# Statistics of the residual one tile per pair, and five other pieces of work at other places, in a four-layer kernel on one core

## The chip, the core and the metric

The kernel runs on one NeuronCore of a Trainium2 chip. The core has a matrix engine (TensorE; PE in the profile, its weight loads PEld), a vector engine (VectorE, DVE), an activation engine (ScalarE, ACT), a general engine (GpSimd, POOL), and the queue of the sync engine (SP), which here issues every DMA. The metric is the time of one execution on the device, in microseconds (us), as the median of the runs shown. Before the change it is 844.3 us.

## The reference

The input is 2 sequences of 512 tokens, 512 wide. Each of four layers adds its normed output to the residual x:

```
x = x + ln(mamba(ln(x)))       # projections to 1024, causal conv of 4 taps, selective scan with 16 states, @ W_out.T
x = x + ln(ffn16(ln(x)))       # gate, up and down weights packed in 4 bits, 1376 inner columns, silu(gate) * up
x = x + ln(attention(ln(x)))   # 16x16 scores of each token, one key and value head
x = x + ln(moe(ln(x)))         # shared expert relu(.)^2 with up and down, and a routed product
# ln(a) = (a - mean(a)) / sqrt(var(a) + 1e-5) along the 512 columns
```

The second layer dequantizes its weights: `w = q * s - (z + 1) * s`, q from `(word >> 4 * (row % 8)) & 15`, with scales s and zero points z of groups of 128 rows.

## The kernel before

A sequence ("half", b = 0 or 1) has four tiles of 128 tokens (t = 0 to 3). There is no scheduler: each engine runs the list of instructions that is written out for it, and semaphores tie the lists together. Four tables or positions in loops set the order. In PSUM four banks hold sums or decays, one holds the scan's output, and three are a ring that all other products of TensorE (items such as `("out", 1, 3)`) go through in one order, so that an item waits until the one three before it has been taken.

**The scan stage** (about 60 to 494 us of the profile) runs 128 pairs. Pair i belongs to chunk cc = i // 8 (128 of the 1024 channels of one half; 16 chunks) and to q = i % 8 in it. For each pair

- ScalarE writes two exponentials of 128x512 to PSUM (`decay`, line 1708), once VectorE is through with pair i-2, whose banks they take;
- GpSimd multiplies `rep_du` by `bc` into `dbu` (line 2142, three buffers), after the scan three pairs back;
- VectorE scans over both (line 1104), and multiplies the states by C (line 1115); for two or three pairs of eight GpSimd does that product (line 2151);
- TensorE sums the states of two pairs (line 881).

Other work is put behind certain pairs. On ScalarE these are copies from PSUM, the steps of the next chunks' dt (lines 1672 to 1678) and, once `out` of half 0 is there, layer norms: behind pairs 90 and 91 `sums(t)` (line 1733) goes over two tiles each of the residual x, with the row sum by the accumulator; behind pair 92 comes `less_mean`, and behind 92 and 93 `squares` (line 1739) of two tiles each; behind 94 `own_root`. Each `sums(t)` waits until GpSimd has added the normed tile to x (line 2180), which it does for two tiles behind pair 87 and for two behind pair 89. `norm_ffn` reads the result behind pair 103.

**The end of the scan stage.** The product with W_out for half 1 has 8 terms, one per chunk. Its first 6 are summed during the scan (`("part", t)`, t = 0 to 3; ScalarE copies them to `obuf`), and the last 2 behind the last scan (`("out", 1, t)`), where VectorE adds both (line 1407).

**The FFN of half 0** (about 505 to 607 us) has 11 steps of 128 inner columns. In step i TensorE does `g` and `u` (12 f16 products of 128x512 each, since operands are split in a high and a low f16 part), and then the 12 products of `down(i-1)`. `g` waits for the weights of step i (`wlo_gu`), `down` for `it_lo` of its step. At the same time VectorE and ScalarE make the weights of the steps to come out of loads of 1.5 MB each (`stage`, four slots; the first three issue freely, `stage(3)` when `("out", 1, 3)` is computed, and `stage(i)` from 4 on when the weights of step i-4 are made). VectorE does in step i: `it` = silu(g) * u (line 1299); unpack of step i+3 (line 1147, waits for its load); `it_lo` (line 1309, waits for the high part from ScalarE); the low weights of step i+2 (lines 1162 and 1164, after ScalarE's high part); scaling for step i+3 (lines 1154 and 1156). At the end of step 0 stand the statistics of the normed `out` of half 1 (lines 1047 and 1050), and at the end of step 4 those of the new residual; at the end of steps 8 to 10 stands the low part of a transposed tile of half 1 (`low_turned`, line 1172). ScalarE does in step i: silu, high part of `it`, high weights of i+2, cast for i+3, then the high part of a transposed tile (`high_turned`, line 1778) and, in steps 1 and 5, the root of the statistics with a table load before and after. TensorE transposes tile t of half 1 at the end of step 7+t (line 652), into the ring bank that the tile before it must have left.

The FFN of half 1 with the attention of half 0 follows (607 to about 703 us), and then the last layer.

Of the kernel before, what the change touches and what calls it, by code (L numbers as in the profile page):

```python
# [48 lines left out]
LOG_EXP = "natural_log_exp_and_others"  # L49

# [37 lines left out]
PARTS = DC - 2  # L88
# [71 lines left out]
def build(nc, x_in, ident_in, meanmat_in, shift_in, shifts_in, w_in, conv_in, par_in, alog_in, wx_in, wdt_in,  # L160
# [15 lines left out]
    with ExitStack() as ctx:  # L176
# [274 lines left out]
        def wait_taken(eng, item):  # L451

            eng.wait_ge(taken_sem(item), ring(item)[1] + 1)
# [184 lines left out]
        def _(pe):  # L638
# [111 lines left out]
            def out_partial(t):  # L750

                item = ("part", t)
                pe.wait_ge(y_taken, DC + PARTS)
                start(item)
                product(item, [(u0[:, c, t * P:(t + 1) * P], wout[:, c, :]) for c in range(PARTS)])\
                    .then_inc(work_ready, 1)

            def out_part(b, t):
# [4 lines left out]
                               for c in range(PARTS * b, DC)])\  # L763
# [271 lines left out]
        def _(dve):  # L1035
# [384 lines left out]
            for i in range(IC):  # L1420
# [5 lines left out]
                ffn_low(0, i)  # L1426
                if i == 2:
# [13 lines left out]
                if i == 0:  # L1441
                    for t in range(NT):
                        wait_taken(dve, ("out", 1, t))
                    stats(("out", 1), [obuf[1][:, t, :] for t in range(NT)])
                if i == 4:
                    dve.wait_ge(out_done, NB * NT)
                    stats(("ffn", 1), x_tiles(1))
                if i > TURN_FIRST:
                    low_turned(1, [i - TURN_FIRST - 1])
# [119 lines left out]
        def _(act):  # L1569
# [287 lines left out]
            for i in range(NPAIR):  # L1857
# [75 lines left out]
                if i in (last + 12, last + 13):  # L1933
                    sums(2 * (i - last - 12))
                    sums(2 * (i - last - 12) + 1)
                if i == last + 14:
                    less_mean()
                    squares(("ffn", 0), 0, x[:, 0, :])
                    squares(("ffn", 0), 1, x[:, 1, :])
                if i == last + 15:  # L1940
                    squares(("ffn", 0), 2, x[:, 2, :])
                    squares(("ffn", 0), 3, x[:, 3, :])
# [4 lines left out]
                if i == last + 16:  # L1947
                    own_root(("ffn", 0), fnmr, fnmr_ready)
# [52 lines left out]
            act.wait_ge(exp_done, NPAIR)  # L2001
            whole(0)
# [4 lines left out]
            for k in range(NB * IC):  # L2007
                b, i = divmod(k, IC)
                ffn_silu(k)
                ffn_high(k)  # L2010
                if k + 2 < IC:
                    high_weights(k + 2)
                if k + 3 < IC:
                    whole(k + 3)
                if TURN_FIRST < k < IC:
                    high_turned(1, [k - TURN_FIRST - 1])
# [293 lines left out]
```

## Time and profile before

| | us |
|---|---|
| median of 3 runs | 844.3 (842.31 to 845.25) |
| profiled execution, its own time | 844.68 |
| its span, first to last instruction | 842.8 |
| TensorE products busy | 692.8 (82%) |
| VectorE busy | 691.4 (82%) |
| GpSimd busy | 493.8 (59%) |
| ScalarE busy | 460.0 (55%) |
| mean granted TensorE clock | 0.904 of full speed |

All times below are of that profiled execution, counted from the start of its span. 1.9 us of its own time lie outside the span. The shares are means over stages of different kinds. A row of a timeline has the start, the busy time and the instruction; what stands in brackets is how long the engine sat idle before it, and whose work ended that.

### The profile page before, as it was taken

The page shows a single profiled execution, that of the slowest core. Times are in us where ns is not written, and L with a number is a line of the kernel's source. Part 1 is how long each engine was busy: PE and PEld are TensorE (multiplying, and loading weights), DVE is VectorE, ACT ScalarE, POOL GpSimd, SP SyncE. Part 2 cuts the span into 40 slices and gives each one's busy share as a digit, 9 for nine tenths or more (in the row PEclk, how much of TensorE's full clock was granted, in tenths as well). Part 3 has the DMA queues.
Part 4 walks back from the last instruction along what each step waited for, and adds up shares of the span by engine and source line. Part 5 has one row for each costly group of instructions (what it writes and reads, how often), then busy time and mean ns, then how long its engine had stood idle before and what let it go on. Part 6 is the DMA issues. An engine that isn't in the chain of part 4 may idle for free. (4 is left out here: it accounts for less than half of the span.)

```text
span 842.8 us, 8287 instructions
## 1 busy us (share of the span) xinstructions
PE 692.8 (82%) x2732; PEld 320.0 (38%) x2732; DVE 691.4 (82%) x700; ACT 460.0 (55%) x772; POOL 493.8 (59%) x258
## 2 busy tenths in 40 slices
PE   5989679998777879366648868997999999999993
PEld 4533123332222323011112223433444546787882
DVE  5779899999999999979999989997265564586668
ACT  3556687797655765856555434765334346323421
POOL 1319999989999999999998920210002005340151
PEclk9999879999968999756858979999999999999998
DMA  9224312331535524533127029870040030000011
GB/s 289 49 74 158 118 37 95 126 124 65 185 103 182 168 75 138 176 124 113 38 100 222 28 76 236 227 210 18 1 150 1 0 100 2 1 0 1 1 51 50
DMA packets 40945, 82.39 MB, mean 98 GB/s; under 512 B 6711, under 2 KB 8160, under 8 KB 40648
## 3 DMA queue, kind: packets, MB, share of 16 engines
q1 hardware_dynamic: 40904, 81.87, 31.0%
q8 instruction: 22, 0.36, 0.2%
q14 instruction: 19, 0.16, 0.1%
HBM read 70.65 MB, written 11.21 MB: 97 GB/s over the span
## 5 line engine op out<-in xcount | busy, mean ns | idle before, releaser
L2142 POOL TENSOR_TENSOR dbu<-rep_du,bc 128x1024 f32<-128x1024 f32 x128 | 299.6, 2366 | 2.3 <-ACT rep_du L1837 1.4
L1708 ACT ACTIVATE psum<-rep_dt,aneg 128x512 f32<-128x512 f32 x256 | 166.2, 682 | 125.2 <-DVE hc L1115 104.8
L1104 DVE TENSOR_TENSOR_SCAN psum<-psum,dbu 128x1024 f32<-128x1024 f32 x87 | 198.8, 2285 | 10.2 <-ACT psum L1708 9.7
L881 PE MATMUL psum<-hc,stk 128*32 128x512 f32 x512 | 87.5, 762 | 58.8 <-POOL hc L2151 30.4
L1115 DVE TENSOR_TENSOR hc<-psum,bc 128x1024 f32<-128x1024 f32 x87 | 106.5, 1224 | 3.4 <-PE psum L881 0.4
L2151 POOL TENSOR_TENSOR hc<-hc,bc 128x1024 f32<-128x1024 f32 x41 | 96.8, 2360 | 8.6 <-DVE hc L1104 8.5
L1104 DVE TENSOR_TENSOR_SCAN hc<-psum,dbu 128x1024 f32<-128x1024 f32 x41 | 93.5, 2281 | 4.7 <-PE psum L881 2.8
L658 PE MATMUL psum<-xf_hi,gu_hi 128*128 128x512 f16 x176 | 67.4, 383 | 1.5 <-ACT sg L1982 1.0
L658 PE MATMUL psum<-xf_hi,gu_lo 128*128 128x512 f16 x176 | 67.2, 382 | 0.0
L658 PE MATMUL psum<-xf_lo,gu_hi 128*128 128x512 f16 x176 | 67.2, 382 | 0.0
L873 PE MATMUL psum<-u,diag 128*32 128x512 f32 x128 | 24.6, 851 | 42.3 <-DVE u L1131 22.9
L881 PEld LDWEIGHTS psum<-hc,stk 128*32 128x32 f32 x512 | 12.9, 122 | 116.7 <-issue 68.4
L2220 POOL TENSOR_TENSOR h<-h 128x512 f32<-128x512 f32 x16 | 19.3, 1208 | 64.5 <-ACT h L2070 63.8
L658 PE MATMUL psum<-xT,w_g 128*128 128x512 f32 x112 | 56.4, 652 | 0.3 <-DVE dt_t L1123 0.3
L1299 DVE TENSOR_TENSOR it<-sg,psum 128x512 f32<-128x512 f32 x22 | 15.1, 685 | 44.3 <-issue 24.8
L1989 ACT CAST it_hi<-it 128x512 f16<-128x512 f32 x22 | 13.6, 620 | 54.6 <-DVE it L1299 54.6
L2184 POOL TENSOR_TENSOR x<-x,obuf 128x512 f32<-128x512 f32 x4 | 8.2, 2076 | 52.2 <-ACT obuf L1766 52.2
L2191 POOL TENSOR_TENSOR w_gate_lo<-w_gate,w_gate_hi 128x32 fp32r<-128x32 f32 x1 | 0.7, 695 | 64.3 <-ACT w_gate_hi L2038 64.3
L2204 POOL TENSOR_TENSOR w_up_lo<-w_up,w_up_hi 128x1024 fp32r<-128x1024 f32 x4 | 9.4, 2378 | 47.4 <-ACT w_up_hi L1974 47.4
L906 PE MATMUL psum<-d_hi,it_hi 128*128 128x512 f16 x88 | 33.3, 379 | 4.6 <-DVE it_lo L1309 4.6
L658 PEld LDWEIGHTS psum<-xT,w_g 128*128 128x128 f32 x112 | 22.4, 208 | 36.4 <-issue 35.1
L658 PE MATMUL psum<-xT,w_x 128*128 128x512 f32 x64 | 31.4, 637 | 3.2 <-ACT u L1636 1.8
(256 smaller groups left out, 1444.5 us busy)
## 6 DMA issues: line engine op xcount, KB each, us to landing
rep_dt<-rep_scratch SPq DMA_DIRECT2D x60, 256.0 KB, 3.3
rep_du<-rep_scratch SPq DMA_DIRECT2D x60, 256.0 KB, 4.2
cw<-c_scratch SPq DMA_DIRECT2D x11, 768.0 KB, 9.4
qw<-qgu_in SPq DMA_DIRECT2D x11, 512.0 KB, 5.3
bc<-bc_scratch SPq DMA_DIRECT2D x16, 256.0 KB, 4.8
rep_scratch<-du_t SPq DMA_DIRECT2D x15, 256.0 KB, 2.0
rep_scratch<-dt_t SPq DMA_DIRECT2D x15, 256.0 KB, 2.3
qw<-qd_in SPq DMA_DIRECT2D x11, 256.0 KB, 7.0
```

The costliest lines, as they stand in the source:

```text
L658: last = pe.matmul(bank(item)[0:rows, cols], lhsT, rhs, start=(n == 0), stop=(n == len(parts) - 1))
L873: last = pe.matmul(y_rows(k), diag[:, k * P // KH:(k + 1) * P // KH], u[b][:, c, :], start=True, stop=False)
L881: last = pe.matmul(y_rows(k), stk[:], hc[:, (i + k // 2) % HCS, k % 2, :], start=False, stop=(s == GN - 1))
L906: last = pe.matmul(psum[:, t, :], v, w, start=(i == 0 and n == 0), stop=(i == IC - 1 and n == 2))
L1104: dve.tensor_tensor_scan(h, a, dbu[:, i % DBS].rearrange("p e t -> p (e t)"), 0.0, ALU.mult, ALU.add)\
L1115: dve.tensor_tensor(hc[:, i % HCS], psum[:, two, :], bc[:, GN + n, :].unsqueeze(1).broadcast_to([P, 2, L]), ALU.mult)\
L1299: dve.tensor_tensor(it[:, k % 2, :], sg[:, k % 2, :], bank(("u", b, i)), ALU.mult)\
L1708: last = act.activation(psum[:, 2 * (i % 2) + e, :], rep_dt[:, cc % 2, k, :], ACT.Exp, scale=aneg[:, k, c, n:n + 1])
L1989: act.copy(it_hi[:, k % 2, :], it[:, k % 2, :]).then_inc(ithi_done, 1)
L2142: pool.tensor_tensor(dbu[:, i % DBS], rep_du[:, cc % 2, k:k + 2, :], bc[:, n, :].unsqueeze(1).broadcast_to([P, 2, L]), ALU.mult).then_inc( ...
L2151: pool.tensor_tensor(hc[:, i % HCS], hc[:, i % HCS], bc[:, GN + n, :].unsqueeze(1).broadcast_to([P, 2, L]), ALU.mult)\
L2220: pool.tensor_tensor(h2[:, k % 2, :], h1[:, k % 2, :], h1[:, k % 2, :], ALU.mult)\
```

## The change

Six pieces of work get another place; only a load of ScalarE's function table is made explicit, and nothing is computed in another way.

1. In the scan stage ScalarE's `sums` go one tile per pair behind pairs 91 to 94, `less_mean` and the `squares` one tile per pair behind 95 to 98, and `own_root` behind 99.
2. `("part", 3)` sums 7 of the 8 terms, and `("out", 1, 3)` the last one alone. The other three tiles keep 6 and 2.
3. ScalarE loads the table set with silu right after the last exponential of the scan stage, and not before the first silu.
4. VectorE's statistics of `out` (half 1) move from the end of step 0 of the FFN to behind `it_lo` of step 1, and those of the residual from the end of step 4 to behind `it_lo` of step 5.
5. `low_turned` of VectorE moves from the end of its step to behind `it_lo`.
6. `high_turned` of ScalarE moves ahead of the high weights.

```diff
-PARTS = DC - 2
+
+
+def parts_of(t):
+
+    return DC - 1 if t == NT - 1 else DC - 2
...
                 ffn_low(0, i)
+                if i > TURN_FIRST:
+                    low_turned(1, [i - TURN_FIRST - 1])
+                if i == 1:
+                    for t in range(NT):
+                        wait_taken(dve, ("out", 1, t))
+                    stats(("out", 1), [obuf[1][:, t, :] for t in range(NT)])
+                if i == 5:
+                    dve.wait_ge(out_done, NB * NT)
+                    stats(("ffn", 1), x_tiles(1))
                 if i == 2:
...
                     scaled(i + 3)
-                if i == 0:
-                    for t in range(NT):
-                        wait_taken(dve, ("out", 1, t))
-                    stats(("out", 1), [obuf[1][:, t, :] for t in range(NT)])
-                if i == 4:
-                    dve.wait_ge(out_done, NB * NT)
-                    stats(("ffn", 1), x_tiles(1))
-                if i > TURN_FIRST:
-                    low_turned(1, [i - TURN_FIRST - 1])
...
-                if i in (last + 12, last + 13):
-                    sums(2 * (i - last - 12))
-                    sums(2 * (i - last - 12) + 1)
-                if i == last + 14:
-                    less_mean()
-                    squares(("ffn", 0), 0, x[:, 0, :])
-                    squares(("ffn", 0), 1, x[:, 1, :])
-                if i == last + 15:
-                    squares(("ffn", 0), 2, x[:, 2, :])
-                    squares(("ffn", 0), 3, x[:, 3, :])
+                if last + 13 <= i < last + 13 + NT:
+                    sums(i - last - 13)
+                if last + 17 <= i < last + 17 + NT:
+                    t = i - last - 17
+                    if t == 0:
+                        less_mean()
+                    squares(("ffn", 0), t, x[:, t, :])
...
-                if i == last + 16:
+                if i == last + 21:
                     own_root(("ffn", 0), fnmr, fnmr_ready)
...
             act.wait_ge(exp_done, NPAIR)
+            act.preload_act_table_set(SILU)
             whole(0)
...
                 ffn_high(k)
+                if TURN_FIRST < k < IC:
+                    high_turned(1, [k - TURN_FIRST - 1])
                 if k + 2 < IC:
                     high_weights(k + 2)
                 if k + 3 < IC:
                     whole(k + 3)
-                if TURN_FIRST < k < IC:
-                    high_turned(1, [k - TURN_FIRST - 1])
```

(`last` is 78, `TURN_FIRST` is 7.) The line numbers of the changed program are 6 or 7 higher at the places below, and those of its VectorE rows 7 higher.

ScalarE's list behind pairs 89 to 94. The `psum<-rep_dt,aneg` rows are the exponentials, two for a pair; `spare,asum<-x` is a `sums`, `spare,avar<-x` a `squares`, `dt_t`, `diag` and `w1t` are work that stays. Before:

```order
L1708 ACTIVATE psum<-rep_dt,aneg 128x512 x6
L1733 ACTIVATE spare,asum<-x 128x512 x2
L1708 ACTIVATE psum<-rep_dt,aneg 128x512 x2
L1672 ACTIVATE dt_t<-psum 128x512
L1733 ACTIVATE spare,asum<-x 128x512 x2
L1708 ACTIVATE psum<-rep_dt,aneg 128x512 x2
L1683 ACTIVATE diag<-ident,par 128x128
L1675 ACTIVATE dt_t<-dt_t 128x512
L1736 ACTIVATE nmean<-asum 128x4
L1739 ACTIVATE spare,avar<-x,nmean 128x512 x2
L1708 ACTIVATE psum<-rep_dt,aneg 128x512 x2
```

With the change:

```order
L1715 ACTIVATE psum<-rep_dt,aneg 128x512 x8
L1679 ACTIVATE dt_t<-psum 128x512
L1740 ACTIVATE spare,asum<-x 128x512
L1715 ACTIVATE psum<-rep_dt,aneg 128x512 x2
L1690 ACTIVATE diag<-ident,par 128x128
L1682 ACTIVATE dt_t<-dt_t 128x512
L1740 ACTIVATE spare,asum<-x 128x512
L1715 ACTIVATE psum<-rep_dt,aneg 128x512 x2
L1685 ACTIVATE dt_t<-dt_t 128x512
L1857 COPY w1t<-psum 128x512
L1740 ACTIVATE spare,asum<-x 128x512
```

Between the exponentials of pairs 91 and 92, where two `sums` stood, now stands one, and it is that of the first tile.

VectorE's list from the end of step 0 of the FFN of half 0 (`w_132` is the scaled weight of step 3). Before:

```order
L1156 TENSOR_TENSOR w_132<-cw_136 128x1536
L1047 BN_STATS bst<-obuf_111 128x6 x4
L1050 BN_AGGR mv<-bst 128x2 x4
L1299 TENSOR_TENSOR it<-sg,psum 128x512
L1147 TENSOR_SCALAR qw_125<-qw_125,shift 128x1536
L1309 TENSOR_TENSOR it_lo<-it,it_hi 128x512
L1162 TENSOR_TENSOR gu_lo<-w_132,gu_hi 128x1024
```

With the change:

```order
L1163 TENSOR_TENSOR w_132<-cw_136 128x1536
L1306 TENSOR_TENSOR it<-sg,psum 128x512
L1154 TENSOR_SCALAR qw_125<-qw_125,shift 128x1536
L1316 TENSOR_TENSOR it_lo<-it,it_hi 128x512
L1054 BN_STATS bst<-obuf_111 128x6 x4
L1057 BN_AGGR mv<-bst 128x2 x4
L1169 TENSOR_TENSOR gu_lo<-w_132,gu_hi 128x1024
```

The eight instructions of the statistics stood ahead of `it`, the unpack and `it_lo` of step 1; now they stand behind these and ahead of the low weights of step 3. The same happens in steps 4 and 5.

VectorE's list in step 8 (`xf_lo` is the low part of the transposed tile 0). Before:

```order
L1299 TENSOR_TENSOR it<-sg,psum 128x512
L1309 TENSOR_TENSOR it_lo<-it,it_hi 128x512
L1162 TENSOR_TENSOR gu_lo<-w_131,gu_hi 128x1024
L1164 TENSOR_TENSOR d_lo<-w_131,d_hi 128x512
L1172 TENSOR_TENSOR xf_lo_142<-psum,xf_hi_140 128x4x128
```

With the change:

```order
L1306 TENSOR_TENSOR it<-sg,psum 128x512
L1316 TENSOR_TENSOR it_lo<-it,it_hi 128x512
L1179 TENSOR_TENSOR xf_lo_142<-psum,xf_hi_140 128x4x128
L1169 TENSOR_TENSOR gu_lo<-w_131,gu_hi 128x1024
L1171 TENSOR_TENSOR d_lo<-w_131,d_hi 128x512
```

`xf_lo` passes the two instructions of the low weights; `xf_hi` on ScalarE passes the two of the high weights in the same way. In steps 9 and 10 no weights are left to be made, and the rows stand as before.

## Rows read from the trace of the kernel before

**Rows 1.** The page, part 1: busy us, share of the span and instructions of each engine.

```profile
PE 692.8 (82%) x2732; PEld 320.0 (38%) x2732; DVE 691.4 (82%) x700; ACT 460.0 (55%) x772; POOL 493.8 (59%) x258
```

**Rows 2.** Windows: start:end and length, busy us (instructions), clock, DMA share, GB/s.

```profile
361.00:395.00 34.00, 20.64 (x56) 4.90 (x54) 28.55 (x18) 22.47 (x48) 33.89 (x18) 0.65 0.28 99
395.00:493.70 98.70, 64.18 (x230) 18.80 (x230) 97.98 (x62) 50.32 (x82) 90.81 (x42) 0.76 0.30 99
607.30:646.30 39.00, 37.64 (x177) 17.11 (x175) 24.49 (x47) 15.91 (x26) 3.42 (x3) 1.00 0.22 81
646.30:807.00 160.70, 157.56 (x763) 109.78 (x764) 99.72 (x185) 66.00 (x118) 40.65 (x30) 1.00 0.05 15
```

**Rows 3.** Timeline of VectorE: the scans of pairs 91 to 94.

```profile
368.11 2.30 DVE L1104 TENSOR_TENSOR_SCAN psum<-psum,dbu 128x1024 f32<-128x1024 f32 x1 [0.48 <-POOL dbu L2142]
...
374.95 2.30 DVE L1104 TENSOR_TENSOR_SCAN psum<-psum,dbu 128x1024 f32<-128x1024 f32 x1 [3.29 <-ACT psum L1708]
...
379.07 2.29 DVE L1104 TENSOR_TENSOR_SCAN hc<-psum,dbu 128x1024 f32<-128x1024 f32 x1 [0.56 <-ACT psum L1708]
...
382.85 2.30 DVE L1104 TENSOR_TENSOR_SCAN psum<-psum,dbu 128x1024 f32<-128x1024 f32 x1 [0.91 <-ACT psum L1708]
```

**Rows 4.** Timeline of ScalarE: the third of the sums, and a read of the accumulator.

```profile
371.64 0.63 ACT L1733 ACTIVATE spare<-x 128x512 f32<-128x512 f32 x1 [3.29 <-POOL x L2180]
372.17 0.19 ACT L1733 ACTIVATION_READ_ACCUMULATOR spare<-x 128x1 f32 x1
```

**Rows 5.** Timeline of GpSimd behind the residual's additions.

```profile
372.73 2.35 POOL L2151 TENSOR_TENSOR hc<-hc,bc 128x1024 f32<-128x1024 f32 x1
375.03 6.98 POOL L2142 TENSOR_TENSOR dbu<-rep_du,bc 128x1024 f32<-128x1024 f32 x3
```

**Rows 6.** Timeline of TensorE: last W_out products, step 1's g, down(1), transpose of tile 1.

```profile
496.65 8.78 PE L658 MATMUL psum<-wout,u 128*128 128x512 f32 x16 [0.81 <-DVE u L1131]
...
511.05 0.39 PE L658 MATMUL psum<-xf_hi,gu_hi 128*128 128x512 f16 x1 [0.43 <-DVE gu_lo L1162]
...
527.38 0.38 PE L906 MATMUL psum<-d_hi,it_hi 128*128 128x512 f16 x1 [1.52 <-DVE it_lo L1309]
...
585.14 0.97 PE L652 MATMUL psum<-ident,obuf 128*128 128x128 f32 x4 [4.40 <-DVE xf_lo L1172]
```

**Rows 7.** Timeline of VectorE in the FFN of half 0, steps 0 to 2.

```profile
516.16 1.02 DVE L1147 TENSOR_SCALAR qw<-qw,shift 128x1536 int32<-128x1536 int32 x1 [0.62 <-DMA cw<-c_scratch]
...
522.10 2.46 DVE L1047 BATCH_NORM_STATS2 bst<-obuf 128x6 f32<-128x512 f32 x4
...
525.01 0.69 DVE L1299 TENSOR_TENSOR it<-sg,psum 128x512 f32<-128x512 f32 x1
...
526.55 0.69 DVE L1309 TENSOR_TENSOR it_lo<-it,it_hi 128x512 f16<-128x512 f32 x1
527.34 1.23 DVE L1162 TENSOR_TENSOR gu_lo<-w,gu_hi 128x1024 f16<-128x1024 f32 x1
...
532.99 0.69 DVE L1299 TENSOR_TENSOR it<-sg,psum 128x512 f32<-128x512 f32 x1 [1.01 <-ACT sg L1982]
```

**Rows 8.** Timeline of VectorE in step 8: low parts of it and of tile 0.

```profile
581.76 0.69 DVE L1309 TENSOR_TENSOR it_lo<-it,it_hi 128x512 f16<-128x512 f32 x1 [0.74 <-DVE it L1299]
...
584.40 0.68 DVE L1172 TENSOR_TENSOR xf_lo<-psum,xf_hi 128x512 f16<-128x512 f32 x1
```

**Rows 9.** Timeline of ScalarE: the table load before the first silu, and xf_hi of tile 0.

```profile
510.27 1.28 ACT L1982 ACT_TABLE_LOAD   x1
...
583.05 0.58 ACT L1778 CAST xf_hi<-psum 128x512 f16<-128x512 f32 x1
```

**Rows 10.** DMA issues of 508 to 509 us: the last transfer of stage(4), us to landing.

```profile
cw<-c_scratch SPq DMA_DIRECT2D x1, 768.0 KB, 14.6
```

**Rows 11.** Windows, TensorE alone: length, busy us, granted clock, DMA share, GB/s.

```profile
406.00:411.70 5.70, 3.03 (x13) 1.00 0.00 0
585.10:588.70 3.60, 3.56 (x11) 0.53 0.00 0
```

More of the change, by code:

```diff
@@ L49 @@
 LOG_EXP = "natural_log_exp_and_others"
+SILU = "silu_and_others"
 POOL_C = ((1, 4, 6), (2, 5))
@@ L752, in out_partial @@
                 item = ("part", t)
-                pe.wait_ge(y_taken, DC + PARTS)
+                pe.wait_ge(y_taken, DC + parts_of(t))
                 start(item)
-                product(item, [(u0[:, c, t * P:(t + 1) * P], wout[:, c, :]) for c in range(PARTS)])\
+                product(item, [(u0[:, c, t * P:(t + 1) * P], wout[:, c, :]) for c in range(parts_of(t))])\
                     .then_inc(work_ready, 1)
@@ L762, in out_part @@
                 product(item, [(gated[b][:, c, t * P:(t + 1) * P], wout[:, c, :])
-                               for c in range(PARTS * b, DC)])\
+                               for c in range(parts_of(t) * b, DC)])\
                     .then_inc(work_ready, 1)
```

## The prediction

> **What bounds the kernel now.** I read the page first. TensorE and VectorE are both busy for 82% of the span [rows 1], so no engine bounds it as a whole and the stages have to be read apart. The windows do that. From 395 to 494 us, in the scan stage, VectorE works for 97.98 of 98.70 us and GpSimd for 90.81: VectorE bounds, with GpSimd 8% behind. From 361 to 395 us it is the other way round: GpSimd 33.89 of 34.00 us, VectorE only 28.55 [rows 2]. That is where the moved statistics of the residual stand. From 607 us on TensorE is the bound, 37.64 of 39.00 us and 157.56 of 160.70 [rows 2]. So whatever is gained before 607 us should reach the end whole, and the change touches nothing behind it.
>
> The waits in the two stages that it does touch are next. In the scan stage the scans of pairs 92, 93 and 94 begin 3.29, 0.56 and 0.91 us late, each for ScalarE's exponentials [rows 3]; 4.8 us in all. The reason is in ScalarE's own list: the third of its `sums` sat 3.29 us until GpSimd had added tile 2 to the residual [rows 4], and the exponentials of pair 92 were queued behind it. In the FFN of half 0 TensorE waits for VectorE: 1.52 us before `down(1)`, and once more the same before `down(5)`, both right behind moved statistics, and 4.40 us before the transpose of tile 1 [rows 6].
>
> **The change part by part.**
>
> *Residual statistics in the scan stage.* The same eight passes are done (0.63 us and a read of 0.19 us for one of the sums [rows 4]), so the work is unchanged and only what queues behind it differs. Behind pair 91 there is now one sum, of tile 0, which has long been added. The sums of tiles 2 and 3 come behind pairs 93 and 94, later than 372.73 us, when GpSimd is through with its additions [rows 5]. None waits. A pair takes VectorE 2.2 us or, with the product by C, 3.5 us; ScalarE has its exponentials and one pass in 2.1 us, so it keeps up. The 4.8 us of waits for ScalarE go. What is late next is GpSimd: the `dbu` of pair 93 is the first of the three that begin at 375.03 and take 6.98 us together, so it is there at 377.4 [rows 5]. The scan of pair 93 began at 379.07 [rows 3], and can begin 1.6 us earlier, not 4.3. From there the scan (2.2) and a short step of VectorE (0.6) follow, so pair 94 starts at 380.3 instead of 382.85 [rows 3]: 2.5 us earlier. Behind it GpSimd has some 8% of room [rows 2], and followed through its list it comes within 0.1 us of holding the scans up once more. I take **2.4 us**. The bounds are 0 (if GpSimd gives nothing back) and 4.8 (if it has room that I don't see). `own_root` comes five pairs later and still four pairs ahead of its reader; it costs nothing.
>
> *One term of the W_out product of tile 3.* The eight products behind the last scan take 8.78 us [rows 6]. The first two run at half rate, so with six at full rate one of these costs 8.78 / 10 = 0.9 us. Moved ahead, it stands in `("part", 3)` in a place where TensorE then idles for some 4 us, and its chunk has long been taken: hidden. Behind the scan it saves TensorE 0.9 us, but `g` of step 1 waits for its low weights at 511.05 in any case [rows 6], so TensorE itself gains nothing. It has another effect: `stage(3)` is issued when this product is done. VectorE's unpack in step 0 waited for just this load until 516.16 [rows 7], and now has it 0.9 us earlier. The gain is **0.9 us**, with 0 as the lower bound if the transfers land no earlier.
>
> *The table load.* 1.28 us go from before the first silu [rows 9]. VectorE would then have `it` of step 0 some 0.6 us earlier, but it waits for the load at 516.16 a little later [rows 7], which hides this: 0 now, 0.6 if that cover were gone.
>
> *Statistics one step later.* They are 2.46 us and the 0.4 behind it: 2.9 us, from 522.10 to the `it` at 525.01 [rows 7]. Without them, and with the 0.9 from above, this `it` starts 3.8 us earlier, at 521.2. The unpack behind it then meets the load of `stage(4)`, issued between 508 and 509 us and landed 14.6 us later, so at 523.2 [rows 10], or 522.4 with the 0.9; it waits 0.6 us. `it_lo` is ready for `down(1)` when TensorE comes, and the 1.52 us of [rows 6] are gone. Then the 2.9 us of statistics follow, and behind them the low weights of step 3, for which TensorE now waits some 0.8 us. On VectorE's chain two things are removed: the 1.01 us before the `it` at 532.99 [rows 7], where ScalarE had to wait for the statistics and then load two tables, and about 0.3 us of short gaps such as that between `it_lo` at 526.55 and the low weights at 527.34, where 0.6 would do [rows 7]. One thing is added, the 0.6 us for the load. Net 0.7. In steps 4 and 5 the same is done with loads that land early: net 1.3. Together **2.0 us**. Bounds: 0, if TensorE's wait for `it_lo` only becomes one for weights, and 3.0, both waits of 1.52.
>
> *The turned tile.* Transpose 1 needs tile 0's ring bank, and this is free when `xf_lo` at 584.40 is through; between it and `it_lo` at 581.76 stand two low-weight instructions [rows 8]. The next start behind `it_lo` is 0.6 us after it, 582.4: **2.0 us** earlier. `xf_hi` has to be there by then; it was at 583.05 [rows 9], behind two casts of 1.5 us which it now passes. The low weights of step 10 come 0.6 us later, more than 10 us ahead of their use. The bounds are 1.5 and 2.0.
>
> *The clock.* Behind that wait of 4.40 us [rows 6] TensorE was granted 0.53 of its clock for 3.60 us [rows 11], the lower of its two levels (1.2 and 2.4 GHz) nearly throughout, which loses 1.7 us. The wait now is 2.4 us. In the window from 406 to 411.7 us TensorE idled for 2.7 us at a stretch, and the granted clock stayed at 1.00 [rows 11]. So I expect it not to fall: **1.7 us**. The bounds are 0 and 1.7. The Trainium skill (TensorE: Matmul & The Clock Gate, the section on the clock gate) says that half rate is the default and that activity, watched in windows that run freely, releases it. By that rule the moment is a matter of chance between executions: the sum would be 1.7 us less in a run where a window falls badly.
>
> The sum is 2.4 + 0.9 + 2.0 + 2.0 + 1.7 = 9.0 us. From the profiled execution's own 844.7 us this gives 835.7; the median of the runs is 0.4 lower, so **835.3 us**.
>
> **The rivals.**
>
> - *GpSimd has more room than I see*, and the scan stage gives all 4.8 us: 835.3 - 2.4 = 832.9 us. Against it stands 33.89 of 34.00 us.
> - *The scan stage gives nothing*, as GpSimd takes the place of ScalarE or the nine passes hold up exponentials of the short pairs: 837.7. For it speaks that one pass and two exponentials nearly fill a pair of 2.2 us.
> - *The clock falls all the same* at 580 us: 837.0. A single pair of numbers speaks against it.
> - *The transfers don't come earlier.* Four are in flight together there, and the load of step 4 took 14.6 us. If the loads bound steps 0 to 2, the 0.9 goes and with it some 0.4 of the first statistics: 836.6.
> - *The statistics now delay the weights by as much*: 837.3.
> - *Slower: TensorE falls to 1.2 GHz in the dense part.* The change makes TensorE's work arrive otherwise, and a stretch of T us at the lower level loses T / 2. From 607 us on the windows show 1.00 throughout [rows 2]. To eat the 9.0 us it takes 18 us of such a stretch, and at 27 us the time is 848.8 us. Nothing in the profile hints at it.
> - *The change does nothing measurable*: the waits are named wrongly, 844. In the scan stage the exponentials' wait is plain, so this needs GpSimd to have been the true cause there as well as in the FFN.
>
> **How the numbers follow.** Chances: my forecast 42 in 100; full gain in the scan stage 8; none there 11; the clock falls 17; the transfers 12; weights delayed 4; slower 3; nothing 3. Two of the lesser misses together reach 839.4, and the best case with a little off is 832. The range is 832.0 to 839.5 us. 0.3% (2.5 us) is about what a measurement of this kernel can tell from no change. All cases but the last two are faster by more: faster 0.94, same 0.03, slower 0.03.
>
> **What would show it.** In the profile after: the scan of pair 92 without a wait, that of pair 93 waiting for GpSimd's `dbu` by 1 to 3 us; the last scan 2.4 us earlier; the unpack of step 0 still waiting for its load, but 0.9 us earlier counted from the last scan; no wait of TensorE for `it_lo` before `down(1)` and `down(5)`, and one under 1 us for low weights before the `g` behind each; TensorE's wait before the transpose of tile 1 down to 2.4 us, and the clock at 1.00 behind it. From 607 us on the stages should be as long as before. I would be wrong if the wait of pair 93 for `dbu` repeats in the pairs that follow, if the transfers of `stage(4)` and `stage(5)` end the waits in steps 1 and 2, or if later stages, which I take over unchanged, give something back.

## The result and the profile after

The changed kernel takes **837.64 us** (median of 4 runs, 835.98 to 837.94), against 844.41 (842.31 to 845.25) for the kernel before on the same chip: a ratio of 0.9923, 95% interval 0.9909 to 0.9937. That is 6.8 us less, where 9.0 were forecast; 837.64 lies in the range of 832.0 to 839.5 and 2.3 us above the point of 835.3. Its profiled execution took 837.52 us with a span of 835.7, so 7.1 us less in the span. The mean granted clock is 0.901 (before 0.904). The ratio is estimated over all runs of both kernels and is not the quotient of the two medians (0.9920 here), so a difference taken from ratios can be up to 1 us away from one taken from medians; below it is said where medians were used.

The page's first part, to be held against [rows 1]: the same work to within 1.5 us on each engine.

```profile
PE 691.4 (83%) x2732; PEld 320.0 (38%) x2732; DVE 690.6 (83%) x700; ACT 459.2 (55%) x772; POOL 493.4 (59%) x258
```

The windows over the same stretches as in [rows 2] (columns as there). VectorE's busy time from 361 to 395 us rose from 28.55 to 30.95: the 2.4 us that it sat idle less. GpSimd is as full there as it was. In the last stage, taken over 161.0 us where it was 160.7, TensorE is busy for 157.91 us where it was 157.56, at a clock of 1.00 in both.

```profile
361.00:395.00 34.00, 20.47 (x64) 4.78 (x62) 30.95 (x20) 22.83 (x45) 33.93 (x19) 0.70 0.29 95
...
639.00:800.00 161.00, 157.91 (x764) 109.73 (x765) 99.76 (x185) 65.96 (x118) 40.80 (x30) 1.00 0.05 16
```

VectorE's scans of pairs 91 to 94, which answer to [rows 3]. The 3.29, 0.56 and 0.91 us for ScalarE are gone, and one wait of 2.36 us for GpSimd stands before pair 93.

```profile
368.29 2.30 DVE L1111 TENSOR_TENSOR_SCAN psum<-psum,dbu 128x1024 f32<-128x1024 f32 x1 [0.49 <-POOL dbu L2147]
371.76 2.29 DVE L1111 TENSOR_TENSOR_SCAN psum<-psum,dbu 128x1024 f32<-128x1024 f32 x1
377.67 2.29 DVE L1111 TENSOR_TENSOR_SCAN hc<-psum,dbu 128x1024 f32<-128x1024 f32 x1 [2.36 <-POOL dbu L2147]
380.45 2.29 DVE L1111 TENSOR_TENSOR_SCAN psum<-psum,dbu 128x1024 f32<-128x1024 f32 x1
```

GpSimd's rows to [rows 5]: its list starts 0.2 us later, as the whole program does in this execution, and is otherwise unmoved. Pair 94 thus starts 2.40 us earlier than before, or 2.6 us counted from that later start.

```profile
375.22 6.97 POOL L2147 TENSOR_TENSOR dbu<-rep_du,bc 128x1024 f32<-128x1024 f32 x3
```

Four more rows of VectorE before the change are wanted as marks: the product of the last scan stage, the add of `("out", 1, 1)`, `it` of step 0 and `it` of step 6.

```profile
495.91 0.69 DVE L1131 TENSOR_TENSOR u<-u,psum 128x512 f32<-128x512 f32 x1 [1.13 <-PE psum L881]
...
502.04 0.69 DVE L1407 TENSOR_TENSOR obuf<-psum,obuf 128x512 f32<-128x512 f32 x1 [1.02 <-PE psum L658]
...
512.19 0.69 DVE L1299 TENSOR_TENSOR it<-sg,psum 128x512 f32<-128x512 f32 x1 [0.60 <-ACT sg L1982]
...
566.57 0.69 DVE L1299 TENSOR_TENSOR it<-sg,psum 128x512 f32<-128x512 f32 x1 [1.01 <-ACT sg L1982]
```

The same marks after, with the rows that answer to [rows 7]:

```profile
493.71 0.69 DVE L1138 TENSOR_TENSOR u<-u,psum 128x512 f32<-128x512 f32 x1 [1.13 <-PE psum L888]
...
501.03 0.69 DVE L1414 TENSOR_TENSOR obuf<-psum,obuf 128x512 f32<-128x512 f32 x1 [2.07 <-PE psum L665]
...
510.50 0.68 DVE L1306 TENSOR_TENSOR it<-sg,psum 128x512 f32<-128x512 f32 x1
...
513.76 1.02 DVE L1154 TENSOR_SCALAR qw<-qw,shift 128x1536 int32<-128x1536 int32 x1
...
519.69 0.68 DVE L1306 TENSOR_TENSOR it<-sg,psum 128x512 f32<-128x512 f32 x1
520.29 1.01 DVE L1154 TENSOR_SCALAR qw<-qw,shift 128x1536 int32<-128x1536 int32 x1
521.22 0.68 DVE L1316 TENSOR_TENSOR it_lo<-it,it_hi 128x512 f16<-128x512 f32 x1
...
529.14 0.68 DVE L1306 TENSOR_TENSOR it<-sg,psum 128x512 f32<-128x512 f32 x1
...
561.27 0.68 DVE L1306 TENSOR_TENSOR it<-sg,psum 128x512 f32<-128x512 f32 x1
```

TensorE's rows to [rows 6]. The 1.52 us before `down(1)` is gone (so is that before `down(5)`), and no wait for weights stands behind it. The wait before the transpose of tile 1 fell from 4.40 to 2.37.

```profile
494.45 9.12 PE L665 MATMUL psum<-wout,u 128*128 128x512 f32 x14 [0.81 <-DVE u L1138]
...
510.04 0.39 PE L665 MATMUL psum<-xf_hi,gu_hi 128*128 128x512 f16 x1 [1.29 <-DVE gu_lo L1169]
...
523.29 0.38 PE L913 MATMUL psum<-d_hi,it_hi 128*128 128x512 f16 x1
...
577.79 0.65 PE L659 MATMUL psum<-ident,obuf 128*128 128x128 f32 x4 [2.37 <-DVE xf_lo L1179]
```

Taking the starts of the same instructions from each other gives where the time came from:

| up to | shift | the step |
|---|---|---|
| `u` at 493.71 | -2.20 | scan stage -2.4, and 0.2 later from the start |
| add at 501.03 | -1.01 | **+1.2 given back** in the W_out products |
| `it` of step 0 at 510.50 | -1.69 | -0.7, of it 0.60 the wait for `sg` |
| unpack at 513.76 | -2.40 | -0.7, of it 0.62 the wait for the load |
| `it` of step 2 at 529.14 | -3.85 | -1.45, first statistics |
| `it` of step 6 at 561.27 | -5.30 | -1.45, second statistics |
| transpose 1 at 577.79 | -7.35 | -2.05, turned tile |
| end | -7.1 | nothing for the clock; 0.2 lost near 700 us |

The windows of TensorE alone for its two stretches at half clock (columns as in [rows 11]): around the W_out products, and behind the transpose of tile 1.

```profile
486.60:500.20 13.60, 9.62 (x23) 0.50 0.34 84
578.70:582.10 3.40, 3.40 (x9) 0.50 0.00 0
```

The same of before, around the W_out products:

```profile
489.80:500.00 10.20, 7.04 (x20) 0.50 0.21 53
```

Both stretches at half clock end near 500 us, though the products now start 2.2 us earlier. Of the time behind that start 3.35 us lay at 1.2 GHz before (496.65 to 500.0) and 5.75 us now (494.45 to 500.2). These are 2.4 us more, and at half clock they cost half of that, the 1.2 us given back in the table. The products of seven terms, 14 recorded ones, take 9.12 us where those of eight, 16 recorded ones, took 8.78 [rows 6].

### The profile page after: what moved, and what is told of

The parts are those of the page before. It is cut to its first block and busy times, and to the rows that moved or that the text cites. A ratio compares the mean times of both kernels' runs of the same rounds, so it can differ in the third digit from the quotient of the medians.

```text
span 835.7 us, 8289 instructions
## 1 busy us (share of the span) xinstructions
PE 691.4 (83%) x2732; PEld 320.0 (38%) x2732; DVE 690.6 (83%) x700; ACT 459.2 (55%) x772; POOL 493.4 (59%) x258
## 5 line engine op out<-in xcount | busy, mean ns | idle before, releaser
L888 PE MATMUL psum<-hc,stk 128*32 128x512 f32 x512 | 85.2, 743 | 60.8 <-POOL hc L2156 37.7
L1993 ACT CAST it_hi<-it 128x512 f16<-128x512 f32 x22 | 13.6, 618 | 51.9 <-DVE it L1306 51.9
```

The source lines that it names most:

```text
L888: last = pe.matmul(y_rows(k), stk[:], hc[:, (i + k // 2) % HCS, k % 2, :], start=False, stop=(s == GN - 1))
```

## Experiments

Twelve kernels were run, each beside the kernel before on the same chip. The diffs show the core of each edit.

### One item at a time

Item 1 alone, the statistics of the residual one tile per pair:

```diff
-                if i in (last + 12, last + 13):
-                    sums(2 * (i - last - 12))
-                    sums(2 * (i - last - 12) + 1)
+                if last + 13 <= i < last + 13 + NT:
+                    sums(i - last - 13)
```

> The kernel before with the residual statistics of the scan stage one tile per pair, and nothing else. My theory, that GpSimd ends the wait that ScalarE ended: the scan of pair 93 waits some 2.4 us for dbu, the last scan ends 2.4 us earlier than in the kernel before, and the time falls by 1.0 to 2.4 us, less where TensorE's clock is low in the W_out products behind the scans. Rival, ScalarE's passes were the whole cause: no wait for dbu, 4.8 us less.

Measured: 843.8 us (842.1 to 844.76, 12 runs) against 843.86 (30 runs), ratio 0.9999 (0.9988 to 1.0009). VectorE's timeline shows the waits gone as in the full change:

```profile
367.01 2.30 DVE L1104 TENSOR_TENSOR_SCAN psum<-psum,dbu 128x1024 f32<-128x1024 f32 x1 [0.51 <-POOL dbu L2139]
370.49 2.29 DVE L1104 TENSOR_TENSOR_SCAN psum<-psum,dbu 128x1024 f32<-128x1024 f32 x1
376.40 2.29 DVE L1104 TENSOR_TENSOR_SCAN hc<-psum,dbu 128x1024 f32<-128x1024 f32 x1 [2.37 <-POOL dbu L2139]
```

This execution was 1.1 us ahead at pair 91 (367.01 against 368.11 in [rows 3]) and 3.7 at pair 94, so 2.6 us were won in the scan stage, and the median shows none. The windows of TensorE say where a part of them went:

```profile
488.20:498.50 10.30, 7.27 (x15) 0.50 0.40 95
580.40:587.20 6.80, 5.32 (x15) 0.50 0.00 0
```

At the product `u` it was 3.5 us ahead (492.43 against 495.91), at the add of `("out", 1, 1)` 2.5: 1.0 us was given back in the W_out products. The stretch at half clock behind the transpose of tile 1 was 6.8 us long where it was 3.4, which cost another 0.9. The span ended 2.2 us earlier than before, so in this execution 1.1 us were won after all; of these 0.7 are the wait for a load in step 0, which only the profile before has (see items 2 and 3 below).

Item 4 alone, VectorE's statistics one step later:

```diff
                 ffn_low(0, i)
+                if i == 1:
+                    for t in range(NT):
+                        wait_taken(dve, ("out", 1, t))
+                    stats(("out", 1), [obuf[1][:, t, :] for t in range(NT)])
```

> The kernel before with the two statistics of VectorE one step later, and nothing else. My theory, that this term was sized too small: the changed kernel's trace gives 1.4 us at each of the two places, so 2.9 us less. Rival, my own term of the prediction: 2.0 us. Rival, the statistics only delay weights: 0.

Measured: 840.55 us (839.39 to 842.08, 7 runs), ratio 0.9968 (0.9955 to 0.9981), 2.7 us less. In its trace VectorE moved by 1.45 us in each of the two places, as in the full change. My expectation of 2.9 us came from the changed kernel's trace; the interval of the ratio (1.6 to 3.8 us) holds both 2.9 and the 2.0 of the prediction, and it is the trace that tells them apart.

Items 5 and 6 alone, the turned tile ahead of the weights on both engines:

```diff
                 ffn_low(0, i)
+                if i > TURN_FIRST:
+                    low_turned(1, [i - TURN_FIRST - 1])
...
                 ffn_high(k)
+                if TURN_FIRST < k < IC:
+                    high_turned(1, [k - TURN_FIRST - 1])
```

> The kernel before with the turned halves (low and high) ahead of the weights of step 10, and nothing else. Theory A, the wait before the transpose of tile 1 shrinks from 4.4 to 2.4 us and TensorE's clock falls behind it all the same in most executions: 2.0 us less, with the lower level of the clock in the window behind it. Rival B, the clock stays up, as I had predicted: 3.7 us less. If it is a matter of where the fall of the clock's windows lies, single runs scatter between the two.

Measured: 841.95 us (838.71 to 843.12, 12 runs), ratio 0.9969 (0.9955 to 0.9983), 2.6 us less. The 12 runs spread over 4.4 us and those of the kernel before over 3.8, so the spread does not show whether the clock stayed up in some of them. The wait before the transpose is 2.37 us, and the clock fell behind it all the same, in TensorE's timeline and windows:

```profile
581.67 1.11 PE L652 MATMUL psum<-ident,obuf 128*128 128x128 f32 x4 [2.37 <-DVE xf_lo L1172]
```

```profile
581.40:584.80 3.40, 3.13 (x10) 0.50 0.00 0
735.00:738.40 3.40, 3.40 (x9) 0.50 0.00 0
```

The second window is a fall in the last layer, which the profile before does not have; it cost this execution 1.6 us of a stretch that no edit touches (the same products ran 3.64 us earlier than before ahead of it and 2.06 behind it).

Item 2 alone, a seventh term in `("part", 3)`:

```diff
-PARTS = DC - 2
+def parts_of(t):
+    return DC - 1 if t == NT - 1 else DC - 2
```

> The kernel before with the seventh term of the W_out product of tile 3 in the partial product, and nothing else. My theory, that the loads of the fourth stage land as much earlier as they are issued: the unpack of step 0 no longer waits 0.6 us for its load, the gain there is 0.6 us, and the time falls by 0.5 us. Rival, the freed 0.9 us is worth what the prediction took alone, 0.9 us. Rival, nothing: TensorE waits for the low weights of step 1 in any case.

Measured: 843.51 us (842.53 to 845.48, 12 runs), ratio 0.9999 (0.9988 to 1.001). Item 3 alone, the table load behind the last exponential:

```diff
             act.wait_ge(exp_done, NPAIR)
+            act.preload_act_table_set(SILU)
```

> The kernel before with the load of the silu table right behind the last exponential, and nothing else. My theory: VectorE's it of step 0 starts up to 0.6 us earlier and then waits as much longer for the load of its unpack; no difference. Rival: the wait for the load isn't what holds step 0, 0.6 us or the whole 1.28 us less.

Measured: 842.85 us (841.95 to 844.93, 12 runs) against 843.99 (17 runs), ratio 0.9993 (0.9983 to 1.0003). Neither can be told from no difference. In its profile the 0.60 us before `it` of step 0 is gone, and the unpack behind it does not wait for its load. That second wait, 0.62 us in [rows 7], is in the profile before alone: the unpack of step 0 starts without one in the profiles of all twelve experiments and in that of the changed kernel, with item 2 and without. Three of these kernels (item 4 alone; items 5 and 6 alone; the needless products below) run the same list as the kernel before up to that unpack, or one that differs in TensorE's needless products only, so the wait belongs to one execution and not to the list. In two profiles of the kernels with needless products an earlier unpack waits for a load, 0.38 and 0.69 us: such waits move about.

### Needless products in the idle stretches

To test what the clock is worth, products whose result is overwritten by the next one with `start=True` fill idle time of TensorE: 3 and 2 of f32 with W_out between the last sums of the scan stage, and f16 ones ahead of the transpose of tile 1 (16 in the kernels without items 5 and 6, 6 in the changed kernel). They change no output.

```diff
+                    if cc == NCH - 1 and s >= 2:
+                        start(("out", 1, 0))
+                        for _ in range(3 if s == 2 else 2):
+                            pe.matmul(bank(("out", 1, 0)), u0[:, 0, 0:P], wout[:, 0, :], start=True, stop=True)
...
+                        if i == TURN_FIRST + 1:
+                            start(("g", 0, i + 1))
+                            for _ in range(16):
+                                pe.matmul(bank(("g", 0, i + 1)), gu_hi[:, i, 0:P], xf_hi[b][:, 0, :], start=True,
+                                          stop=True)
```

In the kernel before:

> The kernel before with needless products on TensorE in three of its idle stretches: 3 and 2 products of W_out while it waits for the last two sums of the scan stage, and 16 f16 products while it waits for the ring bank of transpose 1. Their results are overwritten. They change no wait, only what TensorE did before. Theory clock: the W_out products and step 9 then run at a granted clock of 1.00, and the time falls by 1.7 us at step 9 and up to 1.7 us at W_out, 2 to 3.4 us together. Rival, the clock there follows something else than what TensorE did before: no change, or slower by the work added.

Measured: 840.82 us (839.5 to 842.02, 6 runs) against 844.68 (11 runs), ratio 0.996 (0.9946 to 0.9974): 3.4 us less, at the upper end of what was expected, or 3.9 by the medians. The windows of TensorE show the two stretches at full clock; the first had been at half clock up to 500 us. The last W_out products, 16 recorded ones as before, take 7.13 us and no longer 8.78. These 1.65 us and 1.7 behind the transpose of tile 1 are the 3.4.

```profile
489.50:493.90 4.40, 3.05 (x16) 1.00 0.01 2
580.50:588.70 8.20, 7.26 (x37) 1.00 0.00 0
```

```profile
495.70 7.13 PE L658 MATMUL psum<-wout,u 128*128 128x512 f32 x16 [0.81 <-DVE u L1140]
```

With the same products and item 1:

> The same needless products and the residual statistics of the scan stage one tile per pair. The statistics alone moved the last scan by 2.4 us and the time by nothing that could be measured. Theory clock: the 2.4 us were given back at a low clock, so with the products in both kernels the statistics are worth 2.4 us: this one is 2.4 us below the kernel before with the products. Rival, the 2.4 us are lost in a wait of another engine: no difference between the two.

Measured: 839.24 us (837.0 to 841.33, 6 runs), ratio 0.9938 (0.992 to 0.9956): 1.6 us less than without item 1 by the medians, with intervals that overlap. TensorE's row, to be held against the one above:

```profile
492.99 7.13 PE L658 MATMUL psum<-wout,u 128*128 128x512 f32 x16 [0.81 <-DVE u L1140]
```

At full clock the products take the same 7.13 us and end as much earlier as they start, 2.7 us (0.3 of it from before pair 91): nothing is given back there. Of the 2.7 us, 2.5 last up to the last layer, where this execution has a fall of the clock from 731.8 to 735.2 us that cost 1.6. Less the 0.3, item 1 thus has 2.2 us of the expected 2.4 up to 731 us, and the end of this execution shows less.

In the changed kernel (with `range(6)`):

> The changed kernel with needless products in the idle stretches of TensorE: 3 and 2 of W_out ahead of the last two sums of the scan stage, and 6 f16 ones in the wait before transpose 1. They are overwritten and change no wait. Theory clock, by which the step of my prediction that failed is that of the clock: behind transpose 1 it stays at 1.00 (1.7 us) and the W_out products run at full rate (1 to 2 us), so the time is 2.7 to 3.7 us below the changed kernel, 9.5 to 10.5 below the kernel before. Rival, the missing 2 us are lost in waits: no difference from the changed kernel.

Measured: 833.71 us (831.8 to 837.97, 6 runs) against 843.99, ratio 0.9888 (0.9869 to 0.9908). The windows of its profile:

```profile
493.30:496.70 3.40, 3.24 (x4) 0.50 0.58 160
576.10:582.00 5.90, 5.90 (x29) 1.00 0.00 0
```

Against the changed kernel's trace `it` of step 2 starts 2.3 us earlier (526.88 against 529.14) and the transpose of tile 2 4.0 (584.22 against 588.18), so 1.7 us more behind the transpose of tile 1: 4 us. By the medians it is 3.9, by the ratios 3.0. The first window shows that 3.4 us of the W_out products still ran at half clock; they took 7.86 us for 9.12. The term of 1.7 us for the clock at the transpose exists, but this change does not collect it.

### Other orders

GpSimd's additions one at a time behind pairs 87, 89, 91 and 92, and ScalarE's statistics one pair later, on the changed kernel:

```diff
-                if i in (pair_of(("out", 0, NT - 1)) + 9, pair_of(("out", 0, NT - 1)) + 11):
+                if i in (87, 89, 91, 92):
+                    t = (87, 89, 91, 92).index(i)
```

> The changed kernel with GpSimd's four additions to the residual spread: one each behind pairs 87, 89, 91 and 92 and not two behind 87 and two behind 89; the statistics follow one pair later. My theory, that GpSimd is the next to be late: the 2.4 us before the scan of pair 93 shrink to under 1 us, the 0.5 us before pair 91 go, and the last scan ends some 2 us earlier; of this the time shows 0 to 2 us, by the clock behind it. Rival, the wait for dbu has another cause than the additions (the product by C of pair 90): it stays.

Measured: 840.6 us (839.72 to 842.2, 6 runs), ratio 0.9959 (0.9945 to 0.9974), 3.0 us more than the changed kernel where 0 to 2 less were expected. Pair 93's wait for GpSimd fell from 2.36 to 0.50 us, as the theory of item 1 had it. But the copy of `w1t`, which the edit did not touch, waits for all four additions, and the exponentials are behind it. Pair 94 then waits 6.74 us for these, and the product `u` comes at 496.70 instead of 493.71. VectorE, then ScalarE:

```profile
374.03 2.29 DVE L1111 TENSOR_TENSOR_SCAN hc<-psum,dbu 128x1024 f32<-128x1024 f32 x1 [0.50 <-POOL dbu L2147]
383.64 2.30 DVE L1111 TENSOR_TENSOR_SCAN psum<-psum,dbu 128x1024 f32<-128x1024 f32 x1 [6.74 <-ACT psum L1715]
```

```profile
381.07 0.59 ACT L1857 COPY w1t<-psum 128x512 f32<-128x512 f32 x1 [9.05 <-POOL x L2184]
```

The turned tile first in its step, on the changed kernel:

```diff
             for i in range(IC):
+                if i > TURN_FIRST:
+                    low_turned(1, [i - TURN_FIRST - 1])
                 ffn_times(0, i)
...
+                if TURN_FIRST < k < IC:
+                    high_turned(1, [k - TURN_FIRST - 1])
                 ffn_silu(k)
```

> The changed kernel with the turned halves at the very start of a step, ahead of silu on ScalarE and ahead of it on VectorE. The tile was transposed at the end of the step before, so nothing is waited for. TensorE then never waits before transpose 1: the 2.4 us there go, and with them the low clock behind (1.7 us): 3.5 to 4 us below the changed kernel, some 10 us below the kernel before. Rival, VectorE's 0.6 us more ahead of it and it_lo hold down(7) and down(8) up by as much at each step: 2 us below the changed kernel or less.

Measured: 832.59 us (831.64 to 832.79, 4 runs), ratio 0.986 (0.9842 to 0.9878), 5.1 us less than the changed kernel by the medians, more than the 3.5 to 4 expected. TensorE's timeline and the window behind the transpose: a wait of 0.33 us, and the clock stays.

```profile
575.58 0.66 PE L659 MATMUL psum<-ident,obuf 128*128 128x128 f32 x4 [0.33 <-DVE xf_lo L1179]
```

```profile
574.00:582.00 8.00, 7.67 (x38) 1.00 0.00 0
```

Against the changed kernel's trace the transposes of tiles 1, 2 and 3 start 2.2, 4.3 and 4.8 us earlier, of which 0.2 come from before the edit. 2.0 are the wait, the next 2.1 come with the clock at 1.00 and without the wait of 0.28 us before tile 2, and the last 0.5 without that before tile 3.

That order with the W_out products of the fill:

> The changed kernel with the turned halves at the very start of a step and with the needless W_out products in the last two idle stretches of the scan stage. The first alone took 1.4% off the kernel before. Theory clock: 1 to 2 us more go, some 13.5 us below the kernel before. Rival: behind the W_out products TensorE waits for the low weights of step 1 in any case, so no difference from the turned halves alone, 11.8 us.

Measured: 830.33 us (828.53 to 831.07, 5 runs), ratio 0.9839 (0.9824 to 0.9854), the fastest version of all: 13.7 us below the kernel before by the medians, next to the theory's 13.5 and not the rival's 11.8. The interval of the turned tile alone (0.9842 to 0.9878) overlaps, so the rival is not excluded. TensorE still ran at half clock from 494.0 to 497.4 us, 3.4 us where it had been 13.6.

### Item 1 undone in the changed kernel

The reverse of the first diff, everything else as after the change:

```diff
-                if last + 13 <= i < last + 13 + NT:
-                    sums(i - last - 13)
+                if i in (last + 12, last + 13):
+                    sums(2 * (i - last - 12))
+                    sums(2 * (i - last - 12) + 1)
```

> The changed kernel with item 1 undone: the sums and squares of the scan stage stand again in pairs, as before the change, and everything else as after it. Theory (the 2.4 us of the scan stage are mostly given back when the W_out products fall deeper into the stretch at half clock, as the scan change alone measured 0.9999): undoing it costs 0 to 1 us against the changed kernel's 837.6, so 837.6 to 838.6 us, a ratio to the kernel before of 0.992 to 0.993; the profile shows the last scan 2.4 us later than in the changed kernel, a low-clock stretch around the W_out products of about 10 us and not 13.6, and a difference of about 1 us left at the first step of the FFN. Rival (the gain of the scan stage counts in full once the other edits are there, because what stands behind it is no longer held up by loads or the table): 840.0 us, ratio 0.9951. The wait of pair 92's scan for the exponentials is back at about 3.3 us in both.

Measured: 840.72 us (839.15 to 841.91, 6 runs) against 844.01 (10 runs), ratio 0.9956 (0.9942 to 0.9971). By the number the rival (840.0) is nearer than the theory (837.6 to 838.6): beside the other items, item 1 is worth 0.9956 - 0.9923 = 0.33%, 2.8 us (some 1 to 4.5 by the two intervals). The rival's reason, that the gain counts in full, is not what the profile shows. TensorE's windows:

```profile
492.00:502.20 10.20, 6.51 (x17) 0.50 0.25 65
580.70:584.10 3.40, 3.40 (x10) 0.50 0.00 0
734.30:737.70 3.40, 3.40 (x9) 0.50 0.00 0
```

Against the changed kernel's profile this one runs 1.5 us later from early on, 3.9 behind the scans, and 2.93 at the add of `("out", 1, 1)` (503.97): so the W_out products did give back 0.9 of the 2.4 us, as expected. Less the 1.5 us from before the edit, 1.4 us of item 1 are left at the add and at `it` of step 0 (513.44 against 510.50), where about 1 was expected. The last window is the fall in the last layer again, which brought the difference from 2.8 to 4.4. So the 4.4 us between the two profiles are 1.5 from before pair 91, 1.3 left of item 1, and 1.6 of that fall. 1.4 lies in the interval of 1 to 4.5 as 2.4 does: the times alone can't decide between them.

## Why the prediction was right, and where it was not

**What bounds where** held. GpSimd took ScalarE's place after 2.4 us of 4.8, to the tenth: pair 93 began at 377.67 for a forecast 377.4 plus the later start of 0.2, pair 94 at 380.45 for 380.3. That GpSimd was the next limit is shown by the spread additions, which took its wait from 2.36 to 0.50. The rival in which the scan stage gives all 4.8 us is excluded.

**The step that failed is the clock**: "So I expect it not to fall: 1.7 us". The transpose waited 2.37 us as forecast, and 3.4 us at half clock came all the same, in the changed kernel and with items 5 and 6 alone. The one window from which I argued, 2.7 us idle at full clock [rows 11], was a case and no rule; over the whole scan stage the windows give 0.65 and 0.76 [rows 2], so stretches at the lower level were in sight there. With a wait of 0.93 to 1.07 us (needless products) or 0.33 us (turned tile first) the clock stayed. The Trainium skill (TensorE: Matmul & The Clock Gate, the section on the clock gate) says that the moment varies between runs of one kernel, as the windows run freely. Here the fall came in all four profiles with a wait of 2.37 us, so whether it comes did not vary; how long it lasted did, behind the wait of 4.4 us: 3.4 us in three profiles (before, item 2, item 4) and 6.8 in two (item 1, item 3). The rival "the clock falls all the same" is what came, and it had 17 in 100.

**A clock term I had not seen** stands in the scan stage's gain. "Whatever is gained before 607 us should reach the end whole" is wrong: TensorE was at half clock in the W_out products until 500 us with the change or without, so products that begin 2.2 us earlier run more at half clock, and 1.2 us were given back. By the same marks it was 0.9 us for item 1 within the changed kernel and 1.0 for item 1 alone, and nothing between the two kernels with needless products, where the clock is 1.00: there the same products took 7.13 us, started early or late. What sets the end of the stretch no run shows: it was 500.0 and 500.2 us before and after, but 498.5 with item 1 alone and 502.2 with item 1 undone. What item 1 is worth in the end differs by kernel: 0.1 us alone, 1.6 with the needless products, 2.8 beside the other items, with intervals of 1 to 2 us to each side. The profiles show falls elsewhere that would make up the rest (twice the length at the transpose in the one, the last layer in the others), but for one execution each: that they are the cause in the medians is argued and not shown.

**Mis-sized: the statistics**, 2.9 us for 2.0. Both places gave 1.45; the second was forecast with 1.3, and the first with 0.7 only because of a wait of 0.6 us for the load of `stage(4)`, which did not come: the unpack at 520.29 stands right behind `it`. The last transfer of `stage(4)` was issued at 507.63 us and took 12.2 us, so it had landed at 519.8; I had taken the 14.6 us of one execution [rows 10]. Alone the item measured 2.7.

**Mis-sized: the load and the table.** 0.9 us were forecast for the load and 0 for the table. The trace has 1.4: 0.7 from the table load and as much from the wait for the load. The sentence "0 now, 0.6 if that cover were gone" was the right reading, but the cover was a wait of one execution, and item 2 did not remove it: it is gone without item 2 as well. Over many executions, item 2 is worth 0.1 us (0.9999) and item 3 0.6 (0.9993), neither clear of nothing. The Trainium skill (ScalarE: Activation LUTs, the section on what ACT_TABLE_LOAD costs) gives 1283 ns for the load itself and some 2.7 us for a switch with its drain. The row has 1.28 us [rows 9], as the page has it, and the first silu starts 0.01 us behind it, so no drain shows here; what was won on VectorE is 0.6.

**The turned tile** gave 2.05 us for 2.0, before any change of the clock.

The working thus gave 9.0 with the terms 2.4, 0.9, 2.0, 2.0 and 1.7; the trace has 2.4 - 1.2, 1.4, 2.9, 2.05 and 0, together 7.5, of which the later start and the end leave 7.1. So the misses of 1.7 and 1.2 us and those of 0.5 and 0.9 the other way partly cancel, and that the sum comes within 2.3 us of the measured time is in part luck. The rivals nearest by number, nothing from the scan stage (837.7) and weights delayed (837.3), are not what happened: the profile shows both gains. That the later stages stay as they were held within 0.3 us in this profile, but three others show a fall near 735 us that costs 1.6, a small form of the rival "slower", in a stretch that stands at 1.00 in the profiles of before and after.

**Open.** The five items alone multiply to 0.9928, next to the 0.9923 of all together; without item 1 they multiply to 0.9929, but that kernel measured 0.9956. The gap of 2.3 us is at the edge of what the intervals allow. The profiles of that kernel and of the changed one give item 1 only 1.4 us. Stretches at half clock that come in some executions would explain it, and no run here settles how often each comes.

## What to carry to other kernels

Where TensorE idles between pieces of work, treat the granted clock as a part of the stage: a gain upstream can run into a stretch at half clock and be given back, so look at when that stretch ends, with a row, before passing a gain on whole. Here a wait that was only cut from 4.4 to 2.4 us kept its cost in clock, and one cut to 0.3 us lost it, which made the last two microseconds worth 5.1. And a short wait for a DMA in one profile is no cover and no target, until a second profile shows it too. The same holds for a short stretch at full clock behind an idle one.

## What the runs showed of the hardware that was not expected

- TensorE idle for 2.37 us between dense products was followed by 3.4 us at half clock in the profiles of four kernels (the changed one, items 5 and 6 alone, the spread additions, item 1 undone), while 2.7 us idle in the scan stage was not [rows 11]. The fall cost 1.7 us, by the start of the next transpose with the clock at 1.00.
- Products that compute nothing, 5 of f32 and 16 of f16 in idle time, made the kernel before 0.4% faster (ratio 0.996, 0.9946 to 0.9974) and, with 6 of f16, the changed one 0.35% (0.9923 to 0.9888).
- A fall of the clock for 3.4 us came near 735 us in the middle of the last layer in three profiles of kernels whose edits end 130 us earlier, and in neither the profile before nor after. Each cost 1.6 us.
